# Row maxima of an attention kernel, turned by block transposes on VectorE and transfers through HBM instead of by the matrix engine

## What is computed

```python
x = x + attention(layernorm(x))      # 16 heads of 16 channels, rotary q and k, causal-side linear bias
x = x + layernorm(x) @ W.T + b + (layernorm(x) @ V_r) @ C.T

# attention, for each batch and head
attn = q @ k.T * SCALE + bias        # bias = min(key - query, 0) * slope[head] * 8
w = softmax(attn, axis=-1)           # needs the maximum of each row (query) of attn
out = concat(w @ v) @ proj_w.T + proj_b
```

## Time and profile before

| | |
|---|---|
| median of 3 runs | 2109.35 us (2106.3 to 2109.4) |
| span of the profiled execution | 2108.7 us |
| PE, DVE, ACT, POOL busy | 98%, 88%, 72%, 61% |
| granted TensorE clock, mean | 0.989 |
| DMA, mean | 104 GB/s, 35.5% of the 16 engines by SP's queue |
| DMAs by SP, of the largest groups | 512 num, 256 swapped, 192 at, 128 den |
| DMAs by ACT | 128, `at<-max_t`, 16 KB each |

### The profile page before, as it was taken

One profiled execution on the slowest core, in us unless ns is written; L12 is line 12 of the kernel. 1 busy time (PEld: TensorE's weight loads), 2 busy tenths in 40 slices (PEclk: granted clock), 3 DMA queues, 4 the chain that ended last, 5 costly groups with the idle time before them and its releaser, 6 DMA issues.

```text
span 2108.7 us, 81949 instructions
## 1 busy us (share of the span) xinstructions
PE 2074.9 (98%) x33596; PEld 1193.3 (57%) x33596; DVE 1855.8 (88%) x5459; ACT 1513.9 (72%) x2562; POOL 1296.4 (61%) x1093
## 2 busy tenths in 40 slices
PE   6999999999999999999999999999999999999998
PEld 3455555555555555555555555555555555555554
DVE  7899998988998998999898999998999999999972
ACT  2377777777777777787777777777777777777664
POOL 6357566667565667666666666666766666766512
PEclk8699999999999999999999999999999999999999
DMA  5343333433333433334333334334333334333311
GB/s 156 92 115 102 87 112 105 112 116 104 94 103 107 114 113 105 96 101 124 94 113 109 100 97 121 104 105 123 101 86 115 104 109 121 102 95 104 97 51 39
DMA packets 158935, 218.78 MB, mean 104 GB/s; under 512 B 19072, under 2 KB 104960, under 8 KB 158560
## 3 DMA queue, kind: packets, MB, share of 16 engines
q1 hardware_dynamic: 157280, 211.44, 35.5%
q10 hardware_dynamic: 1280, 2.10, 0.3%
HBM read 36.52 MB, written 16.78 MB: 25 GB/s over the span
## 4 chain that ended last, share of the span: by engine, by line
PE 91%; DVE 1%; ACT 1%; issue 1%; POOL 0%; DVEq 0%
PE ps_s L436 30%; PE ps_o L459 21%; PE ps_misc L413 18%; PE ps_misc L400 12%; PE ps_misc L387 3%; PE ps_misc L478 3%; PE ps_t L446 2%; PE ps_misc L469 2%; DVE junk L648 1%; ACT pt L840 0%; PE ps_t L519 0%; ACT x_res L788 0%; ACT x_res L783 0%; DVE x_hat L684 0%; DVE x_res L633 0%
## 5 line engine op out<-in xcount | busy, mean ns | idle before, releaser
L648 DVE CUSTOM_DVE_ANT_0 junk<-ps_s,alibi 128x512 bf16<-128x512 f32 x2004 | 1302.7, 687 | 185.7 <-PE ps_s L436 153.6
L840 ACT ACTIVATE pt<-ps_t 128x1024 f32<-128x1024 f32 x1024 | 1049.6, 1025 | 450.5 <-DVE ps_t L661 441.4
L446 PE MATMUL ps_t<-at 64*128 64x512 f32 x2048 | 762.2, 451 | 2.3 <-ACT pt L840 2.0
L436 PE MATMUL ps_s<-at 64*128 64x512 f32 x2004 | 757.7, 454 | 3.6 <-DVE row_max L648 2.8
L459 PE MATMUL ps_o<-pt,v_one 128*17 128x128 f32 x16384 | 637.4, 273 | 1.4 <-ACT pt L840 1.3
L459 PEld LDWEIGHTS ps_o<-pt,v_one 128*17 128x17 f32 x16384 | 441.1, 98 | 184.2 <-issue 46.0
L436 PEld LDWEIGHTS ps_s<-at 64*128 64x128 f32 x2004 | 325.6, 184 | 240.9 <-DVE row_max L648 133.4
L661 DVE TENSOR_TENSOR ps_t<-ps_t,diag 128x256 f32<-128x256 f32 x1024 | 435.5, 425 | 14.5 <-PE ps_t L446 14.4
L1006 POOL TENSOR_TENSOR rope_b<-raw,rope_sin 128x512 f32<-128x512 f32 x128 | 164.5, 1285 | 327.3 <-ACT raw L820 323.6
L1022 POOL TENSOR_TENSOR halves<-rope_a,swapped 128x512 fp32r<-128x512 f32 x126 | 159.3, 1287 | 322.8 <-DMA swapped<-rope_b 322.8
L446 PEld LDWEIGHTS ps_t<-at 64*128 64x128 f32 x2048 | 328.1, 184 | 13.9 <-ACT pt L840 8.7
(11 more groups left out here) (105 smaller groups left out, 1801.0 us busy)
## 6 DMA issues: line engine op xcount, KB each, us to landing
at<-halves SPq DMA_DIRECT2D x192, 512.0 KB, 4.0
swapped<-rope_b SPq DMA_DIRECT2D x256, 128.0 KB, 2.6
x_in<-in_L_attn_x_dram SPq DMA_DIRECT2D x32, 512.0 KB, 5.2
num<-o_sb SPq DMA_DIRECT2D x512, 32.0 KB
x_res<-in_L_attn_x_dram SPq DMA_DIRECT2D x32, 512.0 KB, 4.3
out_dram<-x_hat SPq DMA_DIRECT2D x32, 512.0 KB, 5.8
at<-spread_den SPq DMA_DIRECT2D x60, 64.0 KB
at<-max_t ACTq DMA_DIRECT2D x128, 16.0 KB
```

The source lines that it names most:

```text
L436: pe.matmul(scores_bank(n, t), operand(n, 0)[:, t * P:(t + 1) * P], operand(n, 1), start=True, stop=True).then_inc(s_done, 1)
L446: pe.matmul(ps_t[:, j, :], operand(n, 1)[:, j * P:(j + 1) * P], operand(n, 0), start=True, stop=True).then_inc(t_done, 1)
L648: dve.tensor_tensor_reduce(unused, scores_bank(n, t), alibi[:, off:off + N], 1.0, LOWEST, ALU.add, ALU.max, row_max[:, hb % 2, t, hh:hh + ...
L840: act.activation(pt[:, h % 2, 2 * pair:2 * pair + 2, :], ps_t[:, 2 * pair:2 * pair + 2, :], ACT.Exp).then_inc(exp_done, 1)
```

## The change

`max2` is laid out anew, so that a block of 32 columns holds one row group r: part e, head i, block of queries t. DVE transposes `max2` in blocks of 32 x 32 into `max_blocks` (`turn_maxima`), in half 0 of the slot of the split, behind that half's two row maxima and ahead of the diagonal bias. SP then writes `max_blocks` to a tensor in HBM with two DMAs (`park_maxima`), in the same slot, and in the next slot, once they have landed, reads them back with two DMAs into the rows of `at` (`place_maxima`). PE's transposes, ACT's copy and ACT's two DMAs are gone. Both new calls of SP stand in its slot loop behind the load of `x_res` and ahead of `den`, `num` and `swapped`. POOL's rest is now written as float32r.

```diff
--- before.py
+++ after.py
@@ -47,6 +47,8 @@
 PROJ = ((66, (2, 2)), (68, (2, 2)))
 FFN = ((82, (2, 2)), (84, (2, 2)))
 XT, DEN, X2T = (-26, -25), (63, 64), (79, 80)
+
+TURN_HALF = 0
 
 ROTATE = (-11, -9, -4, -1)
 FIRST_SLOT = -21
@@ -158,8 +160,8 @@
         at = sb("at", [P, 2, 2, PAIRS, 2, N], F32R)
         v_one = sb("v_one", [P, 2, T, H, D + 1])
         row_max = sb("row_max", [P, 2, T, 8])
-        max2 = sb("max2", [P, T, 2 * 8])
-        max_t = sb("max_t", [2 * 8, N], F32R)
+        max2 = sb("max2", [P, 2, QUARTER])
+        max_blocks = sb("max_blocks", [P, 2, QUARTER])
         junk = sb("junk", [P, 2, N], mybir.dt.bfloat16)
         pt = sb("pt", [P, 2, T, N])
         o_sb = sb("o_sb", [P, HG, P])
@@ -176,6 +178,8 @@
         ps_misc = ps("ps_misc", [P, 512])
 
 
+
+        max_dram = nc.dram_tensor("max_dram", (2 * NB, 2, QUARTER, P), F32).ap()
 
         weights_loaded = sem("weights_loaded")
         rows_loaded = sem("rows_loaded")
@@ -214,7 +218,7 @@
         max_done = sem("max_done")
         max_high = sem("max_high")
         max_split = sem("max_split")
-        max_turned = sem("max_turned")
+        max_turned, max_parked = sem("max_turned"), sem("max_parked")
         max_placed = sem("max_placed")
         t_done = sem("t_done")
         diag_done = sem("diag_done")
@@ -462,13 +466,6 @@
                 if j == T - 1:
                     ins.then_inc(pv_done, 1)
 
-            def max_rows(hb):
-                bank = misc_bank("max")
-                pe.wait_ge(max_split, hb + 1)
-                for t in range(T):
-                    ins = pe.transpose(bank[0:2 * 8, t * P:(t + 1) * P], max2[:, t, :], ident[:, :])
-                misc_filled(ins, ("max", hb), max_turned, hb + 1)
-
             def spread_denominators(b, kc):
                 bank = misc_bank("den", b, kc)
                 if kc == 0:
@@ -521,7 +518,6 @@
             turn_weights()
             for slot in range(FIRST_SLOT, END_SLOT):
                 n, nt, nv = head_at(slot, 0), head_at(slot, T_LAG), head_at(slot, PV_LAG)
-                hb = half_at(slot, 8)
                 if slot == -12:
                     pe.wait_ge(qkv_scaled, 1)
                 if slot == -8:
@@ -577,8 +573,6 @@
                         b, quarters = due(now, DEN[kc])
                         if b is not None:
                             spread_denominators(b, kc)
-                    if hb is not None and half == 1:
-                        max_rows(hb)
                     if nv is not None:
                         weighted_values(nv, 2 * half)
                         weighted_values(nv, 2 * half + 1)
@@ -650,6 +644,13 @@
 
             def slope_block(h):
                 dve.tensor_scalar(diag[:, h, :], behind, slope8[:, h:h + 1], None, ALU.mult)
+
+            def turn_maxima(hb):
+                dve.wait_ge(max_split, hb + 1)
+                if hb:
+                    dve.wait_ge(max_parked, 32 * hb)
+                dve.transpose(max_blocks[:, :, :].rearrange("p r q -> p (r q)"),
+                              max2[:, :, :].rearrange("p r c -> p (r c)")).then_inc(max_turned, 1)
 
             def diagonal_bias(n, pair):
 
@@ -733,6 +734,9 @@
                         row_maximum(n, 2 * half + 1)
                     if n is not None and 3 <= n < T_LAG:
                         slope_block(2 * (n - 3) + half)
+                    hb = half_at(slot, 8)
+                    if hb is not None and half == TURN_HALF:
+                        turn_maxima(hb)
                     for part in range(2):
                         b = batch_at(slot, (29, 30)[part])
                         if b is not None and half == 1 - part:
@@ -795,23 +799,9 @@
                 dst = v_one[:, b % 2, 2 * u:2 * u + 2, :, :].rearrange("p t h e -> p (t h) e")[:, :, 0:D]
                 act.copy(dst, ps_misc[:, :].rearrange("p (x d) -> p x d", d=D)).then_inc(v_staged, 1)
 
-            def place_max(hb, r):
-
-                b, f = divmod(hb, 2)
-                row = r * HALF + M_ROW
-                dst = at[row:row + STEP + 1:STEP, b % 2, f, :, 0, :]
-                act.wait_ge(max_turned, hb + 1)
-                act.dma_start(dst.bitcast(F32), max_t[8 * r:8 * r + 8, :].bitcast(F32)).then_inc(max_placed, 16)
-
             def empty_bank(now):
 
                 slot, half = divmod(now, 2)
-                hb = half_at(slot, 8)
-                if hb is not None and half == 1:
-                    act.wait_ge(misc_full, full_at["max", hb])
-                    if hb:
-                        act.wait_ge(max_placed, 32 * hb)
-                    act.copy(max_t[:, :], ps_misc[0:2 * 8, :]).then_inc(max_turned, 1)
                 cc = chunk_complete(now)
                 if cc is not None:
                     act.wait_ge(misc_full, full_at["qk", cc])
@@ -874,9 +864,6 @@
                     exponentials(nt, 0)
 
 
-                hb = half_at(slot, 9)
-                if hb is not None:
-                    place_max(hb, 1)
                 empty_bank(2 * slot + 1)
                 b = sooner_at(slot, -19)
                 if b:
@@ -902,9 +889,6 @@
                     act.copy(o_sb[:, :, :], ps_o[:, :, :]).then_inc(o_copied, 1)
                 if nt is not None:
                     exponentials(nt, 1)
-                hb = half_at(slot, 8)
-                if hb is not None:
-                    place_max(hb, 0)
 
         def pool_program():
             pool = nc.gpsimd
@@ -959,12 +943,13 @@
                 pool.wait_ge(max_done, 8 * T * (hb + 1))
                 if hb:
                     pool.wait_ge(max_turned, hb)
-                one = ones[:, :].rearrange("p (a b c) -> p a b c", a=1, b=1).broadcast_to([P, T, 2, PAIRS])
-                src = row_max[:, hb % 2, :, :].rearrange("p t (i r) -> p t r i", r=2)
-                dst = max2[:, :, :].rearrange("p t (r e i) -> p t r e i", r=2, e=2)
-                pool.tensor_tensor(dst[:, :, :, 0, :].bitcast(F32R), src, one, ALU.mult).then_inc(max_high, 1)
+                one = ones[:, :].rearrange("p (a b c) -> p a b c", a=1, b=1).broadcast_to([P, 2, PAIRS, T])
+                src = row_max[:, hb % 2, :, :].rearrange("p t (i r) -> p r i t", r=2)
+                dst = max2[:, :, :].rearrange("p r (e i t) -> p r e i t", e=2, i=PAIRS)
+                pool.tensor_tensor(dst[:, :, 0, :, :].bitcast(F32R), src, one, ALU.mult).then_inc(max_high, 1)
                 pool.wait_ge(max_high, hb + 1)
-                pool.tensor_tensor(dst[:, :, :, 1, :], src, dst[:, :, :, 0, :], ALU.subtract).then_inc(max_split, 1)
+                pool.tensor_tensor(dst[:, :, 1, :, :].bitcast(F32R), src, dst[:, :, 0, :, :], ALU.subtract) \
+                    .then_inc(max_split, 1)
 
             pool.memset(minus_half[:, :], -0.5)
             pool.memset(eps[:, :], C * EPS)
@@ -1054,6 +1039,22 @@
                 sp.dma_start(at[part::STEP, b % 2, f, :, :, :].bitcast(F32).rearrange("x i s n -> x (i s) n"), src) \
                     .then_inc(stacked, 16)
 
+            def park_maxima(hb):
+                sp.wait_ge(max_turned, hb + 1)
+                for r in range(2):
+                    sp.dma_start(max_dram[hb, r].rearrange("c (q x) -> q c x", q=QUARTERS), max_blocks[:, r, :]) \
+                        .then_inc(max_parked, 16)
+
+            def place_maxima(hb):
+
+                b, f = divmod(hb, 2)
+                sp.wait_ge(max_parked, 32 * (hb + 1))
+                for r in range(2):
+                    row = r * HALF + M_ROW
+                    dst = at[row:row + STEP + 1:STEP, b % 2, f, :, 0, :]
+                    sp.dma_start(dst.bitcast(F32), max_dram[hb, r].rearrange("(e i t) q -> e i (t q)", e=2, i=PAIRS)) \
+                        .then_inc(max_placed, 16)
+
             def clear_max(b):
                 zeros = no_max.rearrange("x (o n) -> x o n", o=1).broadcast_to([M_ROWS, KC * PAIRS, N])
                 for r in range(2):
@@ -1097,6 +1098,12 @@
                     if b:
                         sp.wait_ge(x2t_done, KC * b)
                     sp.dma_start(x_res[:, :, :], x[b].rearrange("(t p) c -> p t c", p=P)).then_inc(res_loaded, 16)
+                hb = half_at(slot, 8)
+                if hb is not None:
+                    park_maxima(hb)
+                hb = half_at(slot, 9)
+                if hb is not None:
+                    place_maxima(hb)
                 gg = group_at(slot, PV_LAG + 4)
                 if gg is not None:
                     b, g = divmod(gg, G)
```

## The result

The changed kernel takes 2216.8 us (median of 4 runs, 2211.4 to 2218.2) against 2109.2 us: a ratio of 1.051, 95% interval 1.048 to 1.053. The forecast was 2205 us, slower. Its profiled execution was the shortest of the four, with a span of 2209.7 us, 101.0 us over that of before.

A forecast was written before the change was run, and what follows sets the result against it. PE (98% busy) and DVE were each taken as nearly the bound, half slot by half slot. Waits for the placing of 64, 24 and 8 us, with parts 1 and 2 cancelling, add 96 to 2108.7: 2205 us, range 2140 to 2290.

The forecast's parts named there:

- Part 3: SP's queue: placing issued behind parking, nine issues and x_res lands late; PE waits 2.2 us with x_res, 64 us in all.
- The reason given for 14.2: Half batch with x_res: placing alone would land at 13.9 us, but shares x_res's queue, which lands at 14.2 (9.9 + 4.3).
- The other half batch: Half batch without x_res: placing lands at 13.2 us, PE wants it at 12.4 and waits 0.8 us, 24 us over 30.
- parts 1 and 2: Transposes leaving PE and block transpose coming to DVE: 6 us gain and 6 us loss cancel; bounds -10 to +25 us.
- The start: First three half batches, where halves are shorter: PE's waits of 1.5, 2.8 and 3.9 us, 8 us in all.
- Part 1: Four transposes of the maxima leave PE's half slot: at most 9.6 us gained, about 0.1 us a piece, 6 us.
- part 2: Block transpose comes to DVE, 64 of 0.2 us: about 0.1 us each exposed on average, 6 us lost.
- I count nothing: SP's den, num, swap and stacking go out up to 2.7 us later: 0 us; without PE's wait 0.3 us.

The follow-up runs named there:

- e10_extra_issue: Changed kernel with one more parking transfer per half batch, issued by SP ahead of the other two: 2276.3 us, ratio 1.080 to the kernel before.
- e6_park_act: Changed kernel with parking issued by ACT, placing left with SP behind the load of x_res: 2124.4 us, ratio 1.007 to the kernel before.
- e5_both_act: Changed kernel with parking and placing both issued by ACT instead of SP: 2115.1 us, ratio 1.003 to the kernel before.
- e2_place_ahead: Changed kernel with SP issuing the placing ahead of the load of x_res, not behind it: 2188.6 us, ratio 1.037 to the kernel before.
- e7_turn_twice: Changed kernel with parking and placing issued by ACT, and each DVE block transpose made twice: 2117.8 us, ratio 1.005 to the kernel before.
- e4_one_transpose: Kernel before with three of the four PE transposes of the maxima left out and all maxima placed as 0: 2111.5 us, ratio 1.0008.
- e1_place_act: Changed kernel with only the two placing transfers issued by ACT, in the middle of the next slot: 2155.5 us, ratio 1.020 to the kernel before.

## Why the prediction was right

**Part 3** held in its mechanism and in its larger term. SP begins to park at 2.1 us (2.25 forecast), x_res goes out at 9.8 (9.9), the last placing at 11.2 (11.2), PE goes on at 14.22 (14.2): 63.9 us of 64. e10_extra_issue, e6_park_act and e5_both_act each change only which issues stand in SP's list, and the wait moves with them. The reason given for 14.2 holds in part. x_res landed 4.3 us after its issue in the middle, at 14.1, and the placing with it; but e2_place_ahead shows that being behind it on the queue cost 0.25 us on average. With the placing ahead it still took 2.8 us from the last issue to the first exponent scores, where it lands in 2.3 us without that load. That the sum met 14.2 to 0.02 us is in part luck.

**The other half batch** was oversized: last placing at 10.5 us as forecast, but landed 2.3 us later, not 2.7, and PE, which wants it at 12.54, goes on at 12.94 on average and not at 13.2. Of its 0.54 us, 0.14 is parts 1 and 2 (12.54 with both on ACT against 12.40; the second transpose of e7_turn_twice added 0.12), 0.40 the wait: 15 us, not 24. The start was 8.3 us longer against 8 forecast, but it took 186.7 to 192.0 us in the kernels whose placing ACT issues, so this agreement shows little.

**Parts 1 and 2** were to cancel, and do: 2.1 us over 57 half batches. Part 1's 6 us of gain did not come as such, nor 6 us of loss from part 2: with both on ACT there were 4.0 us of loss and 1.9 us of gain, and e4_one_transpose gave back 0.2 us. That PE's removed work is worth nearly nothing is shown by e4_one_transpose, and it was the waits of both kinds between PE and DVE, not PE's 98%, that said so.

**What was missing** is the clock: PE's granted clock fell after ten of the pauses, 14.5 us in the profiled execution. The terms that were forecast, 96 us, came to 87 us (63.9, 15.1 and 8.3); the rest with x_res, which was not, added 15.7 us. The two misses have opposite signs, and that 101 us came out so near 96 is luck to that extent.

**The step that was wrong without harm**: "I count nothing" for what SP issues after the parking. I followed swap to the stacking and not on to den of the fourth slot, for which DVE waits. It is worth 41 us as soon as PE's own wait is gone (e1_place_act), and stood behind it all along.

The Trainium skill (DMA: Bandwidth & Descriptors, Issuing engines are not separate DMA queues) says that spreading issues over engines saves only the sequencer's time, usually small. The mechanism is what these traces show, the size is not: that time and what followed from it, the lower clock too, was nearly all of the loss, 102 us between the changed kernel and that with both on ACT. Its section Queues, rings and completion order has the descriptors in one issuer's ring taken in order on each DMA engine; the 0.25 us that the placing lost behind x_res agrees.

## What to carry to other kernels

When a transfer moves to another queue, write out that queue's list around it with a pitch for each issue (0.63 us here), and the time at which its result is wanted. Then follow everything behind it up to where it is awaited, even where another wait would cover it: the cover is what one removes first. And where two engines release each other half slot by half slot, work taken from the busier one is worth only what the other one's next release allows; it pays when something is moved into the gap (7 us in the steady part here).

## What the runs showed of the hardware

- PE stood idle for 1.0 to 2.7 us ahead of the first exponent scores of the 29 half batches with x_res in the changed kernel. In ten of them 3.4 us at 1.2 GHz followed, which cost 1.45 us each. With one more issue it stood for 2.0 to 3.3 us, and 25 of 29 were followed by such a stretch. The ten had pauses of 1.6 to 2.7 us, the other 19 of 1.0 to 2.3 us: longer ones did it more often, but between 1.6 and 2.3 us both kinds occur, and what decides there stays open. Filling the pause with matmuls that nothing needs kept the clock at 2.4 GHz.
- A 16 KB transfer in pieces of 128 bytes to HBM held SP for 0.58 us and had landed within 2.4 us; the read back landed 2.3 us after its issue began.
- The end of the kernel takes 126 to 128 us after the same slot in seven of the twelve profiled executions and 135 to 142 us in the other five; each of these five, and none of the seven, has a stretch of 20.5 us at the lower clock near the end. The one trace of the kernel before has 126 us. Whether this makes the spread of its runs, 2103 to 2119 us, is not shown.
